# Query and key projections in two waves with held-back FFN steps between them, a second LayerNorm moved behind the next projections, and Sqrt on ScalarE in place of a Newton square root on VectorE

## The chip, the cores and the metric

One Trainium2 chip, all 8 cores, one launch. Each core computes one element of the batch (4096 rows of 1024 channels) and reads all weights itself; the cores don't talk to each other. The metric is the device time in microseconds (us) of the slowest core.

## What is computed

One transformer layer of the post-LayerNorm kind: linear attention (16 heads of 64, chunks of 128 rows, a running state S and z), residual and LayerNorm, then a mixture of 8 experts (each a 1024x1024 matrix, softmax gate, best two kept), residual and LayerNorm.

```python
q = phi(x @ Wq.T + bq); k = phi(x @ Wk.T + bk); v = x @ Wv.T + bv      # phi = elu + 1
for each chunk of 128 rows, per head:
    scores = tril(q k^T)
    out    = (scores v + q S) / sum(q * (cumsum(k) + z))
    S += k^T v;  z += sum(k)
x = layernorm(x + out @ Wo.T + bo)
gates = softmax(x @ gate_w.T + gate_b); top 2 of 8
x = layernorm(x + sum over the top 2 of gate_e * (x @ expert_w[e].T + expert_b[e]))
```

layernorm subtracts the mean and divides by sqrt(variance + 1e-5), with no learned scale.

## The kernel before

**Superchunks.** The 4096 rows of a core are worked through in 8 superchunks of 512 rows, numbered s = 0 to 7, each with four chunks of 128 rows, c = 0 to 3. All instructions are written out by hand, in one order per engine; `B.wait` and `B.waits` put semaphore waits into an engine's queue, and an engine runs its queue strictly in order. So the order in which the Python code calls `B.op` is the order in which each engine works.

**One superchunk** is four stages:

1. `proj_core` (lines 366 to 472). `proj_qk` computes Q, then K, transposed: for each of 8 slices k of the contraction, 8 matmuls (f = 0 to 7) of 512 columns, so that 64 matmuls (L377) fill all eight halves of the four PSUM tiles `quad` 0 to 3 (q0 to q3 in the rows). Only when the last slice is done does the evacuation begin: per f, ScalarE computes Exp (L393) and Relu (L398) of the half into `etmp` and `etmp2`, of which there are two each, and VectorE combines them (L404) into `qt_bf` or `kt_bf`. K needs the same eight halves, so its first matmul waits for Q's evacuation (line 375). Then K is transposed on TensorE (L426) and copied by VectorE (L435), and V is computed for four chunks (L449, bias L455) and evacuated by ScalarE (L465).
2. The scan over four chunks: `scores_part` (L554, masked by VectorE at L574), `sz_part` (state update, VectorE L626 to L644), `numden_div` (L670 and L675 on TensorE, L686 and L691 on VectorE), and, one chunk behind, `tail_chunk` (output projection L735, residual L755, first LayerNorm L761 to L770) and `tail_b` (transposes L787, their evacuation L795 on ScalarE, the gate: maximum L811, Exp L815, reciprocal L819, the bias term L859 and L871). `build_zmask` (ScalarE, L519) and `build_qz` (VectorE, L532) prepare masked copies of K and Q.
3. `x_stream(s + 1)`: the next superchunk's rows are loaded by POOL's queue and cast by VectorE (L361).
4. `ffn_drain`: 32 expert steps in the order expert 0 chunks 0 to 3, expert 1 chunks 0 to 3, and so on (e6,2 below is expert 6, chunk 2). A step is 16 matmuls of 512 columns (L886) into q0 or q1, alternately, and one VectorE instruction that multiplies by the gate and adds into `x1f` (L900). Then `ln2_out` (lines 929 to 956): for each of the four chunks, statistics (L937 to L943), inverse root (`rsqrt_dve`), normalisation (L947) and the output DMA from POOL's queue.

**The inverse root.** `rsqrt_dve` (lines 474 to 510) is 13 instructions on 128x1 tiles on VectorE: it adds epsilon (L482), guesses by integer arithmetic and makes two Newton steps (L485 to L506), and copies (L509). Both LayerNorms use it, 64 times in all.

**Weights.** There are 12 matrices of 2 MB in bf16 (0 Wq, 1 Wk, 2 Wv, 3 Wo, 4 to 11 the experts), and three buffers `wb` for them. `free_and_feed(mat)` frees a buffer when TensorE is done with a matrix and starts the next load into it, always three matrices ahead: the end of expert 5 starts the load of the next Wq, the end of expert 6 that of Wk, the end of expert 7 that of Wv. In superchunk 0 the matrices come as f32, in halves, through `wb2`, are cast by VectorE (L259) and ScalarE (L262) and stored to DRAM; from superchunk 1 on they are read back as bf16. Wq and Wk come in 8 pieces of 256 KB, one per slice k, even ones from SP's queue and odd ones from POOL's, and each queue waits until its last piece has landed before it issues the next:

```python
for k in range(KB):
    eng = "SP" if k % 2 == 0 else "POOL"
    cn = (f"dwl{slot}" if k % 2 == 0 else f"dwm{slot}")
    B.wait(eng, cn, B.val(cn))
    v = dma(eng, cn, wb[slot][:, k * 1024:(k + 1) * 1024],
            descr[m * 128:(m + 1) * 128,
                  k * 1024:(k + 1) * 1024])
    wpieces[m][k] = [(cn, v)]
```

Of the kernel before, what the change touches and what calls it, by code (L numbers as in the profile page):

```python
# [9 lines left out]
AF = mybir.ActivationFunctionType  # L10
# [11 lines left out]
KB = 8  # L22
# [66 lines left out]
def build():  # L89
# [276 lines left out]
    def proj_core(s):  # L366
        def proj_qk(mat, dstbf, donearr, bias_col):
            src = wb[wslot[mat]]
            vpe_f = [None] * KB
            for k in range(KB):  # L370
                B.waits("PE", wpieces[mat][k])
                B.wait("PE", "cdv", xt_cast[k])
                if k == 0:
                    for f in range(KB):
                        B.waits("PE", qwait(f // 2, (f % 2,)))
                for f in range(KB):
                    fn = lambda e, src=src, k=k, f=f: e.matmul(  # L377
                        quad[f // 2][:, (f % 2) * 512:(f % 2 + 1) * 512],
                        src[:, k * 1024 + f * 128: k * 1024 + (f + 1) * 128],
                        xt_bf[:, k * 512:(k + 1) * 512],  # L380
                        start=(k == 0), stop=(k == KB - 1))
                    if k == KB - 1:
                        vpe_f[f] = B.op("PE", fn, inc="cpe")
                    else:
                        B.op("PE", fn)
            for f in range(KB):
                qi, hh = f // 2, f % 2
# [3 lines left out]
                B.wait("ACT", "cpe", vpe_f[f])  # L391
# [18 lines left out]
            free_and_feed(mat)  # L410
# [299 lines left out]
    def tail_chunk(s, c, attn_evs):  # L710
# [57 lines left out]
        vrsq = rsqrt_dve(mnv[j][:, 1:2], rstd[j][:], rsq[j], [("cdv", vagg)])  # L768
        B.wait("DVE", "cdv", vrsq)
# [141 lines left out]
    ffn_qi = [0]  # L911

# [19 lines left out]
    def ln2_out(s):  # L932
        for c in range(CPS):
# [10 lines left out]
            vrsq2 = rsqrt_dve(mnv2[:, 1:2], rstd2[:], rsq[2], [("cdv", vagg)])  # L944
            B.wait("DVE", "cdv", vrsq2)
# [18 lines left out]
    fed_b2 = [False]  # L964
    for s in range(nsc if stage >= 1 else 0):
        proj_core(s)
        xtbf_free[0] = [("cpe", B.val("cpe"))]
# [36 lines left out]
        if stage >= 4:  # L1004
            ffn_drain(s)
# [4 lines left out]
        if stage >= 5:  # L1010
            ln2_out(s)
# [76 lines left out]
```

How the kernel before makes its waits and increments, by code:

```python
    def wait(self, eng, cname, val):  # L56
        if val is None or val <= 0:
            return
        w = self.waited[eng]
        if w.get(cname, 0) >= val:
            return
        w[cname] = val
        h = self.ctr[cname][0]
        self.streams[eng].append(lambda e, h=h, v=val: e.wait_ge(h, v))
# [14 lines left out]
        def run(e, fn=fn, h=h, k=k):  # L79
            fn(e).then_inc(h, k)
```

## Time and profile before

| what | value |
|---|---|
| median of 2 runs | 3003.82 us (2966.64 to 3041.0) |
| the profiled execution, whole | 2970.23 us |
| its span, first to last instruction, slowest core | 2968.7 us |
| spans of the other seven cores | 2951.6 to 2967.4 us |
| TensorE (PE) busy | 1916.2 us, 65% |
| VectorE (DVE) busy | 1106.4 us, 37% |
| ScalarE (ACT) busy | 405.4 us, 14% |
| DMA traffic | 304.01 MB, mean 102 GB/s |

The profile is of one execution, on core 5. All times in the rows are microseconds from the start of that core's span unless marked ns. PE is TensorE's matmuls, PEld its weight loads, DVE VectorE, ACT ScalarE, POOL and SP the two engines whose queues issue the DMAs. L377 is line 377 of the kernel. `out<-in` gives the tiles written and read, without buffer numbers. The bracket at the end of a timeline row is how long the engine stood idle before it, and which instruction ended that.

### The profile page before, as it was taken

The page shows a single profiled execution, that of the slowest core. Times are in us where ns is not written, and L with a number is a line of the kernel's source. Part 1 is how long each engine was busy: PE and PEld are TensorE (multiplying, and loading weights), DVE is VectorE, ACT ScalarE, POOL GpSimd, SP SyncE. Part 2 cuts the span into 40 slices and gives each one's busy share as a digit, 9 for nine tenths or more (in the row PEclk, how much of TensorE's full clock was granted, in tenths as well). Part 3 has the DMA queues.
Part 4 walks back from the last instruction along what each step waited for, and adds up shares of the span by engine and source line. Part 5 has one row for each costly group of instructions (what it writes and reads, how often), then busy time and mean ns, then how long its engine had stood idle before and what let it go on. Part 6 is the DMA issues. An engine that isn't in the chain of part 4 may idle for free.

```text
span 2968.7 us, 27823 instructions; the slowest of 8 cores (2951.6 to 2968.7 us)
## 1 busy us (share of the span) xinstructions
PE 1916.2 (65%) x10144; PEld 926.1 (31%) x10144; DVE 1106.4 (37%) x2224; ACT 405.4 (14%) x525; POOL 142.4 (5%) x265
## 2 busy tenths in 40 slices
PE   2355545565796549774696648964597646966495
PEld 0132222232342324332242323423243322423242
DVE  0233312433343433534334333434334333343434
ACT  1321110221003100131002200031001310022000
POOL 1000000100000000100000000000001000000000
PEclk8676777876897669886797768986698767977698
DMA  6630365410342113420243113420134202431031
GB/s 170 221 114 15 138 231 221 153 65 8 117 162 91 57 55 127 160 74 12 85 147 137 50 35 115 151 99 36 57 142 142 79 8 92 147 131 50 36 114 57
DMA packets 63356, 304.01 MB, mean 102 GB/s; under 512 B 8172, under 2 KB 8428, under 8 KB 43766
## 3 DMA queue, kind: packets, MB, share of 16 engines
q1 hardware_dynamic: 34326, 163.80, 16.6%
q0 software_dynamic: 28896, 138.43, 12.6%
q8 instruction: 83, 1.36, 0.2%
q14 instruction: 51, 0.42, 0.1%
HBM read 260.26 MB, written 41.94 MB: 102 GB/s over the span
## 4 chain that ended last, share of the span: by engine, by line
PE 52%; DVE 18%; DMA 10%; issue 10%; ACT 8%; DVEq 1%; POOL 0%; ACTq 0%; SPq 0%; POOLq 0%
PE q L886 27%; PE q L735 6%; DMA wb<-ewT 4%; PE q L449 4%; PE q L377 4%; DMA xtl<-xT 3%; PE q L741 2%; PE q L455 2%; ACT etmp L393 2%; PE q L554 2%; PE q L787 1%; ACT wb L262 1%; DVE x1f L755 1%; DVE x1f L871 1%; DVE S_f L626 1%
## 5 line engine op out<-in xcount | busy, mean ns | idle before, releaser
L886 PE MATMUL q<-wb,x1t_bf 128*128 128x512 bf16 x4096 | 927.4, 391 | 134.9 <-DVE x1f L900 63.6
L886 PEld LDWEIGHTS q<-wb,x1t_bf 128*128 128x128 bf16 x4096 | 408.6, 100 | 656.6 <-issue 201.6
L900 DVE SCALAR_TENSOR_TENSOR x1f<-q,w_all,x1f 128x1024 f32<-128x1024 f32 x256 | 328.2, 1283 | 546.5 <-PE q L886 546.5
L377 PE MATMUL q<-xt_bf,wb 128*128 128x512 bf16 x1024 | 245.4, 404 | 216.8 <-ACT etmp L398 165.0
L735 PE MATMUL q<-wb,attnTb 128*128 128x512 bf16 x512 | 172.9, 513 | 79.2 <-ACT attnTb L726 79.2
L377 PEld LDWEIGHTS q<-xt_bf,wb 128*128 128x128 bf16 x1024 | 103.9, 103 | 357.7 <-issue 253.3
L393 ACT ACTIVATE etmp<-q,bqc_s 128x512 f32<-128x512 f32 x64 | 45.2, 707 | 986.9 <-PE q L377 899.2
L554 PE MATMUL q<-qt_bf,ktz 128*128 128x128 bf16 x512 | 53.3, 287 | 173.3 <-DVE qtz L532 173.3
L196 POOL DMA_DIRECT2D wb<-escr x126 | 67.1, 533 | 1759.4 <-PE q L886 782.3
L755 DVE TENSOR_TENSOR x1f<-q,x0c 128x1024 f32<-128x1024 f32 x32 | 39.2, 1224 | 287.4 <-PE q L741 287.4
L574 DVE TENSOR_TENSOR msc_bf<-q,maskT_f 128x1024 bf16<-128x1024 f32 x64 | 75.4, 1220 | 186.6 <-PE q L554 186.6
L787 PE MATMUL q<-id_f,x1f 128*128 128x128 f32 x256 | 58.7, 406 | 128.1 <-DVE x1f L770 75.3
L449 PE MATMUL q<-wb,xt_bf 128*128 128x512 bf16 x512 | 119.9, 388 | 19.5 <-DVE ktm_bf L435 19.5
L735 PEld LDWEIGHTS q<-wb,attnTb 128*128 128x128 bf16 x512 | 61.7, 125 | 183.0 <-issue 163.4
L554 PEld LDWEIGHTS q<-qt_bf,ktz 128*128 128x128 bf16 x512 | 46.2, 132 | 181.6 <-issue 181.6
L259 DVE CAST wb<-wb 128x4096 bf16<-128x4096 f32 x12 | 27.5, 2293 | 197.5 <-DMA wb<-ewT 104.9
L404 DVE SCALAR_TENSOR_TENSOR kt_bf<-etmp 128x512 bf16<-128x512 f32 x64 | 44.3, 693 | 148.3 <-ACT etmp L398 148.3
L519 ACT ACTIVATE ktz<-kt_bf,pmask_s 128x1024 bf16<-128x1024 bf16 x64 | 70.0, 1140 | 203.1 <-PE q L554 196.9
L795 ACT ACTIVATE x1t_bf<-q 128x1024 bf16<-128x1024 f32 x32 | 32.6, 1019 | 449.1 <-PE q L787 449.1
L787 PEld LDWEIGHTS q<-id_f,x1f 128*128 128x128 f32 x256 | 49.9, 222 | 135.2 <-issue 135.2
L426 PE MATMUL q<-id_bf,kt_bf 128*128 128x128 bf16 x256 | 36.6, 295 | 67.1 <-DVE kt_bf L404 67.1
L449 PEld LDWEIGHTS q<-wb,xt_bf 128*128 128x128 bf16 x512 | 48.4, 99 | 95.5 <-issue 45.0
(85 smaller groups left out, 1590.7 us busy)
## 6 DMA issues: line engine op xcount, KB each, us to landing
wb<-escr SPq DMA_DIRECT2D x70, 1024.0 KB, 5.0
wb<-escr POOLq DMA_DIRECT2D x70, 1024.0 KB, 7.0
wb<-ewT SPq DMA_DIRECT2D x16, 2048.0 KB
escr<-wb SPq DMA_DIRECT2D x12, 2048.0 KB, 8.2
xtl<-xT POOLq DMA_DIRECT2D x64, 256.0 KB, 3.3
x0c<-x POOLq DMA_DIRECT2D x32, 512.0 KB, 5.0
out<-osb POOLq DMA_DIRECT2D x32, 512.0 KB, 2.9
wb<-escr SPq DMA_DIRECT2D x56, 256.0 KB, 3.3
```

The lines of the kernel that those rows point to most:

```text
L196: return B.op(eng, lambda e, o=out_ap, i=in_ap: e.dma_start(o, i), inc=cname, k=16)
L377: fn = lambda e, src=src, k=k, f=f: e.matmul(quad[f // 2][:, (f % 2) * 512:(f % 2 + 1) * 512], src[:, k * 1024 + f * 128: k * 1024 + (f + ...
L393: va = B.op("ACT", lambda e, qi=qi, hh=hh, et=et, bc=bc: e.activation(et[:], quad[qi][:, hh * 512:(hh + 1) * 512], AF.Exp, bias=bc), inc=" ...
L449: B.op("PE", lambda e, src=src, k=k, c=c, qi=qi, hh=hh: e.matmul(quad[qi][:, hh * 512:(hh + 1) * 512], xt_bf[:, k * 512 + c * 128: k * 512 ...
L519: vkz = B.op("ACT", lambda e, c=c, par=par, mcol=mcol: e.activation(ktz[:].rearrange("p (h w) -> p h w", w=128)[:, par::2, :], kt_bf[:].re ...
L554: fn = lambda e, h=h, f=f, c=c, qi=qi, hh=hh: e.matmul(quad[qi][:, hh * 128:(hh + 1) * 128], ktz[:, h * 128:(h + 1) * 128], qt_bf[:, f * 5 ...
L574: vm = B.op("DVE", lambda e, half=half, qi=qi: e.tensor_tensor(msc_bf[:, half * 1024:(half + 1) * 1024].rearrange("p (h w) -> p h w", w=12 ...
L735: B.op("PE", lambda e, src=src, k=k, hh=hh, j=j: e.matmul(quad[0][:, hh * 512:(hh + 1) * 512], attnT_bfp[j][:, k * 128:(k + 1) * 128], src ...
L755: vres = B.op("DVE", lambda e, j=j, c=c: e.tensor_tensor(x1f[:, c * 1024:(c + 1) * 1024], quad[0][:], x0c[j][:], ALU.add), inc="cdv")
L787: fn = lambda e, f=f, c=c: e.transpose(quad[0][:, f * 128:(f + 1) * 128], x1f[:, c * 1024 + f * 128: c * 1024 + (f + 1) * 128], id_f32[:])
L886: fn = lambda e, src=src, k=k, c=c, qi=qi, hh=hh: e.matmul(quad[qi][:, hh * 512:(hh + 1) * 512], x1t_bf[:, c * 1024 + k * 128: c * 1024 + ...
L900: e.scalar_tensor_tensor(x1f[:, c * 1024:(c + 1) * 1024], quad[qi][:], w_all[:, c * 8 + e_i: c * 8 + e_i + 1], x1f[:, c * 1024:(c + 1) * 1 ...
```

## The change

Three things are changed.

- **Two waves.** `proj_qk` now computes the eight output blocks in two waves of four, both in q2 and q3. After a wave its four blocks are evacuated (`emit_phi`, the old code), and `ffn_drain` emits up to two expert steps.
- **Held-back steps and the second LayerNorm.** At the end of a superchunk, except the last, six expert steps are left in the queue (e6,2, e6,3 and e7,0 to e7,3); they come out in the next superchunk's projections, two after each of the first three waves. `ln2_out` of superchunk s is then called after the whole of `proj_core(s + 1)`, ahead of its scan.
- **Sqrt.** In both LayerNorms `rsqrt_dve` gives way to a Sqrt with epsilon as bias on ScalarE and a reciprocal on VectorE, with a wait in each direction.

```diff
@@ -367,28 +367,37 @@
...
+            for wv in range(2):
+                fs = range(wv * 4, wv * 4 + 4)
+                for k in range(KB):
+                    B.waits("PE", wpieces[mat][k])
+                    B.wait("PE", "cdv", xt_cast[k])
+                    if k == 0:
+                        for f in fs:
+                            B.waits("PE", qwait(2 + (f % 4) // 2, ((f % 4) % 2,)))
+                    for f in fs:
+                        fn = lambda e, src=src, k=k, f=f: e.matmul(
+                            quad[2 + (f % 4) // 2][
+                                :, ((f % 4) % 2) * 512:((f % 4) % 2 + 1) * 512],
+                            src[:, k * 1024 + f * 128: k * 1024 + (f + 1) * 128],
+                            xt_bf[:, k * 512:(k + 1) * 512],
+                            start=(k == 0), stop=(k == KB - 1))
+                        if k == KB - 1:
+                            vpe_f[f] = B.op("PE", fn, inc="cpe")
+                        else:
+                            B.op("PE", fn)
+                for f in fs:
+                    emit_phi(mat, dstbf, donearr, bias_col, f, vpe_f[f])
+                ffn_drain(s_cur[0], limit=2)
+            free_and_feed(mat)
+
+        def emit_phi(mat, dstbf, donearr, bias_col, f, vpe):
+            if True:
+                qi, hh = 2 + (f % 4) // 2, (f % 4) % 2
...
@@ -765,8 +773,13 @@
...
-        vrsq = rsqrt_dve(mnv[j][:, 1:2], rstd[j][:], rsq[j], [("cdv", vagg)])
-        B.wait("DVE", "cdv", vrsq)
+        B.wait("ACT", "cdv", vagg)
+        vsq = B.op("ACT", lambda e, j=j: e.activation(
+            sdev[j][:], mnv[j][:, 1:2], AF.Sqrt, bias=eps_c[:, 0:1]), inc="cac")
+        B.wait("DVE", "cac", vsq)
+        vrs = B.op("DVE", lambda e, j=j: e.reciprocal(rstd[j][:], sdev[j][:]),
+                   inc="cdv")
+        B.wait("DVE", "cdv", vrs)
...
@@ -941,8 +955,13 @@
...
-            vrsq2 = rsqrt_dve(mnv2[:, 1:2], rstd2[:], rsq[2], [("cdv", vagg)])
-            B.wait("DVE", "cdv", vrsq2)
+            B.wait("ACT", "cdv", vagg)
+            vsq = B.op("ACT", lambda e: e.activation(
+                sdev2[:], mnv2[:, 1:2], AF.Sqrt, bias=eps_c[:, 0:1]), inc="cac")
+            B.wait("DVE", "cac", vsq)
+            vrs = B.op("DVE", lambda e: e.reciprocal(rstd2[:], sdev2[:]),
+                       inc="cdv")
+            B.wait("DVE", "cdv", vrs)
...
@@ -962,8 +981,14 @@
...
     for s in range(nsc if stage >= 1 else 0):
+        s_cur[0] = s
         proj_core(s)
+        if pend_ln2[0] is not None and stage >= 5:
+            ffn_drain(pend_ln2[0])
+            ln2_out(pend_ln2[0])
+            pend_ln2[0] = None
...
@@ -1002,13 +1027,18 @@
...
-            ffn_drain(s)
+            hold = 6 if s + 1 < nsc else 0
+            ffn_drain(s, limit=max(0, len(ffnq) - hold))
...
-            ln2_out(s)
+            if s + 1 < nsc:
+                pend_ln2[0] = s
+            else:
+                ffn_drain(s)
+                ln2_out(s)
```

The waves' matmuls are L379 in the changed kernel, the expert steps L899 with L913 on VectorE, the transposes of K L434, V L457 and L463, the new Sqrts L777 (first LayerNorm) and L959 (second), their reciprocals L780 and L962, the normalisation of the second L966, the mask L582, masked K copies L527, V's evacuation L473 and the cast of S L649.

TensorE around the projections of a superchunk from the second on, before: the 32 expert steps (512 matmuls), Q and K (128), the transposes, V's first chunk and its bias.

```order
L886 MATMUL q<-wb,x1t_bf 128x512 x512
L377 MATMUL q<-xt_bf,wb 128x512 x128
L426 MATMUL q<-id_bf,kt_bf 128x128 x32
L449 MATMUL q<-wb,xt_bf 128x512 x16
L455 MATMUL q<-bv_s,ones_r 128x512 x2
```

And now, at the same place:

```order
L899 MATMUL q<-wb,x1t_bf 128x512 x416
L379 MATMUL q<-xt_bf,wb 128x512 x32
L899 MATMUL q<-wb,x1t_bf 128x512 x32
L379 MATMUL q<-xt_bf,wb 128x512 x32
L899 MATMUL q<-wb,x1t_bf 128x512 x32
L379 MATMUL q<-xt_bf,wb 128x512 x32
L899 MATMUL q<-wb,x1t_bf 128x512 x32
L379 MATMUL q<-xt_bf,wb 128x512 x32
L434 MATMUL q<-id_bf,kt_bf 128x128 x32
```

26 expert steps stand before Q; the other six stand in pairs behind the first wave of Q, the second wave of Q and the first wave of K, and nothing stands between the second wave of K and the transposes.

VectorE from the masked copy of Q to the cast of the state in chunk 0 of such a superchunk, before (the second LayerNorm stood ahead of Q's L404, outside this piece):

```order
L532 TENSOR_SCALAR qtz<-qt_bf,pmask_s 128x8x128 x2
L435 COPY ktm_bf<-q 128x1024 x4
L574 TENSOR_TENSOR msc_bf<-q,maskT_f 128x1024 x2
L626 TENSOR_TENSOR S_f<-q,S_f 64x16x64
L631 TENSOR_TENSOR S_f<-q,S_f 64x16
L644 CAST Sbf<-S_f 64x1040
```

And now, from the last chunk of that LayerNorm to the same cast:

```order
L951 BN_STATS lnst<-x1f 128x6
L953 BN_STATS lnst<-x1f 128x6
L957 BN_AGGR mnv<-lnst 128x2
L962 RECIPROCAL rstd<-sdev 128x1
L966 TENSOR_SCALAR osb<-x1f,mnv,rstd 128x1024
L582 TENSOR_TENSOR msc_bf<-q,maskT_f 128x1024 x2
L634 TENSOR_TENSOR S_f<-q,S_f 64x16x64
L639 TENSOR_TENSOR S_f<-q,S_f 64x16
L652 CAST Sbf<-S_f 64x1040
```

All four chunks of the second LayerNorm (five instructions each) now stand between the copies of K and the first mask of the scan.

ScalarE at the same place, now, with the semaphores waited for (cpe counts TensorE, cdv VectorE):

```order
L527 ACTIVATE ktz<-kt_bf,pmask_s 128x8x128 [waits cdv]
L527 ACTIVATE ktz<-kt_bf,pmask_s 128x8x128
L473 ACTIVATE vext_bf<-q 128x16x64 [waits cpe] x4
L959 ACTIVATE sdev<-mnv,eps_c 128x1 [waits cdv] x4
L527 ACTIVATE ktz<-kt_bf,pmask_s 128x8x128 [waits cpe]
L527 ACTIVATE ktz<-kt_bf,pmask_s 128x8x128
L649 ACTIVATE Sbf<-S_f 64x1040 [waits cdv]
```

The four Sqrts are new; they stand behind the evacuation of all four chunks of V and ahead of the masked copy of K for chunk 1.

## Rows read from the trace of the kernel before

**Rows 1.** The page: span, and DMA issues (KB each, median us to landing).

```profile
span 2968.7 us, 27823 instructions; the slowest of 8 cores (2951.6 to 2968.7 us)
...
wb<-escr POOLq DMA_DIRECT2D x70, 1024.0 KB, 7.0
```

**Rows 2.** Windows, expert steps and scan: length, busy PE, PEld, DVE, ACT, POOL, PEclk, DMA.

```profile
760.00:885.00 125.00, 115.82 (x515) 51.16 (x514) 45.00 (x41) 0.00 (x0) 10.16 (x20) 0.95 0.38 130
...
968.00:1102.00 134.00, 64.77 (x509) 38.89 (x507) 58.53 (x147) 20.52 (x27) 4.52 (x9) 0.65 0.14 51
```

**Rows 3.** Timeline of TensorE, superchunk 2: start, duration, instructions, idle time before.

```profile
884.88 13.97 PE L377 MATMUL q<-xt_bf,wb 128*128 128x512 bf16 x64 [1.61 <-DVE x1f L900]
916.80 16.42 PE L377 MATMUL q<-xt_bf,wb 128*128 128x512 bf16 x64 [17.95 <-ACT etmp L398]
...
942.17 2.85 PE L426 MATMUL q<-id_bf,kt_bf 128*128 128x128 bf16 x25 [0.89 <-DVE kt_bf L404]
...
965.43 1.98 PE L455 MATMUL q<-bv_s,ones_r 1*128 1x512 f32 x4
...
970.84 0.19 PE L670 MATMUL q<-vext_bf,msc_bf 128*128 128x65 bf16 x1 [1.01 <-ACT ktz L519]
```

**Rows 4.** Timeline of VectorE, the same stretch.

```profile
883.45 1.28 DVE L900 SCALAR_TENSOR_TENSOR x1f<-q,w_all,x1f 128x1024 f32<-128x1024 f32 x1 [2.17 <-PE q L886]
884.65 0.68 DVE L937 BATCH_NORM_STATS2 lnst<-x1f 128x6 f32<-128x512 f32 x1
...
908.70 1.29 DVE L404 SCALAR_TENSOR_TENSOR qt_bf<-etmp 128x512 bf16<-128x512 f32 x2
...
941.33 0.69 DVE L404 SCALAR_TENSOR_TENSOR kt_bf<-etmp 128x512 bf16<-128x512 f32 x1 [0.47 <-ACT etmp L398]
...
968.07 2.36 DVE L574 TENSOR_TENSOR msc_bf<-q,maskT_f 128x1024 bf16<-128x1024 f32 x2 [22.26 <-PE q L554]
...
972.47 0.21 DVE L686 RECIPROCAL rden<-q 128x8 f32<-128x8 f32 x1
```

**Rows 5.** Timeline of ScalarE, the same stretch.

```profile
909.48 0.69 ACT L393 ACTIVATE etmp<-q,bqc_s 128x512 f32<-128x512 f32 x1 [9.62 <-DVE qt_bf L404]
...
931.87 0.69 ACT L393 ACTIVATE etmp<-q,bkc_s 128x512 f32<-128x512 f32 x1 [15.21 <-PE q L377]
...
967.51 1.03 ACT L465 ACTIVATE vext_bf<-q 128x1024 bf16<-128x1024 f32 x1 [4.44 <-PE q L455]
```

**Rows 6.** Timeline of POOL's queue: first and fourth of its pieces of Wq.

```profile
856.24 0.54 POOL L196 DMA_DIRECT2D wb<-escr  x1 [13.35 <-PE q L886]
...
868.46 0.54 POOL L196 DMA_DIRECT2D wb<-escr  x1 [3.29 <-DMA wb<-escr]
```

**Rows 7.** Timelines of VectorE and ScalarE in the tail of chunk 0, superchunk 2.

```profile
993.21 0.21 DVE L766 BATCH_NORM_AGGREGATE mnv<-lnst 128x2 f32<-128x12 f32 x1
...
997.00 0.81 DVE L770 TENSOR_SCALAR x1f<-x1f,mnv,rstd 128x1024 f32<-128x1024 f32 x1
...
1006.53 0.17 DVE L811 TENSOR_REDUCE negm<-q 128x1 f32<-128x8 f32 x1 [2.49 <-PE q L807]
...
1006.85 0.27 ACT L815 ACTIVATE eg<-q,negm 128x8 f32<-128x8 f32 x1 [1.22 <-DVE negm L811]
...
1007.31 0.16 DVE L819 RECIPROCAL rg<-sg 128x1 f32<-128x1 f32 x1 [0.61 <-ACT eg L815]
```

**Rows 8.** Timeline of ScalarE: the only table load of the program.

```profile
44.36 1.28 ACT L262 ACT_TABLE_LOAD   x1 [44.36 <-DMA wb<-wqT]
45.65 3.62 ACT L262 ACTIVATE wb<-wb 128x4096 bf16<-128x4096 f32 x1
```

**Rows 9.** Timelines of VectorE and TensorE where superchunk 1 begins.

```profile
505.44 2.29 DVE L259 CAST wb<-wb 128x4096 bf16<-128x4096 f32 x1 [26.08 <-DMA wb<-ewT]
...
574.35 15.29 PE L377 MATMUL q<-xt_bf,wb 128*128 128x512 bf16 x64 [27.29 <-ACT etmp L398]
```

**Rows 10.** Timeline of ScalarE in superchunk 0: the cast of Wo's first half.

```profile
126.12 3.62 ACT L262 ACTIVATE wb<-wb 128x4096 bf16<-128x4096 f32 x1 [4.46 <-DMA wb<-woT]
```

More of the change, by code:

```diff
@@ L369, in proj_qk @@
             vpe_f = [None] * KB
[L370 to L387, printed above, removed]
+            for wv in range(2):
[24 more added lines that the diff above has]
+                qi, hh = 2 + (f % 4) // 2, (f % 4) % 2
                 et = e_tmp[f % 2]
@@ L390, in proj_qk @@
                 bc = bias_col[:, f:f + 1]
-                B.wait("ACT", "cpe", vpe_f[f])
+                B.wait("ACT", "cpe", vpe)
                 B.waits("ACT", etmp_free[f % 2])
@@ L409, in proj_qk @@
                 etmp2_free[f % 2] = [("cdv", vd)]
-            free_and_feed(mat)
         proj_qk(0, qt_bf, qt_done, bqc_s)
@@ L911, in build @@
     ffn_qi = [0]
+    s_cur = [0]
     def ffn_drain(s, limit=None):
@@ L964, in build @@
     fed_b2 = [False]
+    pend_ln2 = [None]
     for s in range(nsc if stage >= 1 else 0):
+        s_cur[0] = s
         proj_core(s)
+        if pend_ln2[0] is not None and stage >= 5:
+            ffn_drain(pend_ln2[0])
+            ln2_out(pend_ln2[0])
+            pend_ln2[0] = None
         xtbf_free[0] = [("cpe", B.val("cpe"))]
```

## The prediction

> **What bounds the kernel now.** I read four views in this order: the windows by stage, the timeline of TensorE for one whole superchunk, those of VectorE and ScalarE under it, and POOL's queue. The windows show two kinds of stage [rows 2]. In the expert steps TensorE is busy for 115.82 of 125 us at a granted clock of 0.95, nearly all of it at 2.4 GHz; a step costs 1.28 + 2.17 = 3.45 us [rows 4], and nothing but TensorE matters. In the scan it is busy for 64.77 of 134 us at 0.65, a mixture of 1.2 and 2.4 GHz: there one chain runs through TensorE, VectorE and ScalarE in turn, and every microsecond on it counts.
>
> Between them stand the projections. Q takes 13.97 us, then TensorE waits 17.95 us for the evacuation, and K takes 16.42 us instead of 13.97, since its first matmuls run at the lower clock after the wait [rows 3]. ScalarE's own work for Q would take some 10 us; it stood still for 9.62 us, because both temporaries were full and VectorE had not begun to combine them [rows 5]. VectorE was in the second LayerNorm of the superchunk before, from 884.65 to 908.70, 24.05 us or 6.01 per chunk, and only then came to L404 [rows 4]. So the wait belongs to two things, the LayerNorm ahead in VectorE's queue and the eight blocks that are freed only at the end.
>
> **Part 1, waves and held-back steps, superchunks 2 to 7.** Before: six steps earlier than the end of the experts, the step e6,1 is done at 883.45 - 0.16 - 6 x 3.45 = 862.6 (0.16 us is about the hop from TensorE to VectorE). From there to the end of K at 916.80 + 16.42 = 933.2 are 70.6 us. After: four waves of 13.97 / 2 = 6.98 and six steps of 3.45, 48.6 us. A wave's evacuation is covered: eight K blocks take from 931.87 to 941.33 + 0.69, 10.15 us [rows 4, 5], 1.16 for each block after the first, so four take about 5.5 us, under 6.9 us of expert steps that write q0 and q1. The VectorE parts of those steps queue behind the evacuation, but the next use of q0 and q1 is a wave away.
>
> The cover has one hole. Wq is loaded when expert 5 is done. Its pieces go one by one in each queue: POOL's first is issued at 856.24, its fourth at 868.46 [rows 6], 4.07 us apart, so the last pair lands at 872.5. Before, Q began 12 us later and saw none of it. Now its first wave begins at 862.6 and wants slices 6 and 7 at 862.6 + 6 x 0.87 = 867.8: a stall of 4.7 us. Wk is loaded from the end of e6,3 and wanted 19 us later (a wave, two steps, six slices), against four pieces of 4.07 = 16.3 us: hidden. Gain: 70.6 - 48.6 - 4.7 = 17.3 us.
>
> Behind the second wave of K only four blocks are left instead of eight, 4 x 1.16 = 4.6 us less, minus 0.9 because the evacuation of a shorter wave begins nearer to its end: 3.8 us gained before the last transposes [rows 3].
>
> **Part 2, the second LayerNorm moved.** VectorE is nearly idle during V (22.26 us before the mask [rows 4]), which looks like free room. But ScalarE's order puts the four Sqrts behind V's last evacuation, which ends at 967.51 + 1.03 = 968.5 [rows 5]. VectorE can do the statistics of chunk 0 and then waits under the whole of V; all else comes after, and ahead of the first mask, which started at 968.07. What that costs needs the length of a round trip. From VectorE to ScalarE the hop is 1006.85 - 1006.70 = 0.15; a small ScalarE instruction 0.27; the way back is not seen alone (the row behind Exp has another small read between), so 0.1; reciprocal 0.16; 0.1 more: 0.78 us in place of 997.00 - 993.42 = 3.58 [rows 7]. So a chunk takes 6.01 - 2.80 = 3.2 us. The first also pays a table load, 1.28 us with the next instruction 0.01 us behind it [rows 8]: 1.28, then 0.63 for Sqrt, way back and reciprocal, and 0.71 for the normalisation: 2.6 us. LayerNorm ends at 968.5 + 2.6 + 3 x 3.2 = 980.7, the mask starts 12.8 us late. VectorE's next recip, 972.47, was its own queue's time and not TensorE's (970.84) [rows 3, 4], so all 12.8 us are on the chain. Bounds: 0 if the Sqrts ran under V, which the queue's order forbids; 24 at the old 6.01 per chunk. I take 12.8. The output DMAs and the x0c loads behind them on POOL's queue come later too, but x0c is wanted some 20 us after that.
>
> **Part 3, Sqrt in the tails.** Gain 2.80 us per chunk on the chain. Cost: Exp (gate, and phi) is loaded; Sqrt needs a load, and the next Exp another. The load of rows 8 waited for its data like the instruction behind it, so I place both on the chain, 1.28 each. In chunk 0 of superchunks 1 to 7 the Sqrt finds its table loaded: 2.80 - 1.28 = 1.52; in the other chunks 2.80 - 2.56 = 0.24. Sum 2.2 us a superchunk, 1.0 in superchunk 0. Bounds per load: 0 (hidden ahead of a wait) and 2.3 (the load, and a pipe that must first empty for as long as the longest neighbour, 1.03 [rows 5]); 1.28 is the row itself. There are 65 new loads: 8 a superchunk and one at the end.
>
> A rule speaks against this part. The trace shows 1.28 us and then the next instruction at once [rows 8]. The Trainium skill (ScalarE: Activation LUTs, What ACT_TABLE_LOAD costs) gives the same 1.28 for the load but adds a drain of 1.38 us to every switch of set. By that rule my sum would be 65 x 1.38 = 90 us longer; the one load seen here fell on an idle engine, and no row shows a switch between two sets.
>
> **Sum.** Superchunks 2 to 7: 17.3 + 3.8 - 12.8 + 2.2 = 10.5 each, 63. Superchunk 1: the last cast of expert 7 ends at 507.7, then Wq's pieces, 4 x 4.07 + 0.5, one slice, three waves and six steps: 507.7 + 16.8 + 0.9 + 20.9 + 20.7 = 567.0 against 574.35 + 15.29 = 589.6 [rows 9]; 22.6 + 3.8 - 12.8 + 2.2 = 15.8. Superchunk 0 has no steps to fill with: its K ends about 8 us later, Wo's cast on ScalarE had 4.46 us of room [rows 10], so 3 us lost, 1 won in the tails. The last LayerNorm, at the open end: 4 x 2.80 - 1.28 = 9.9. Together 63 + 15.8 - 2 + 9.9 = 86.7 us. The profiled execution took 2970.2 us (span 2968.7 [rows 1]): 2970.2 - 86.7 = 2883.5, say 2884. The median of the runs shown, 3003.82, lies 34 us above it and is the middle of two runs 74 us apart; the forecast is for an execution like the profiled one.
>
> **Rivals.** A measurement of this kernel tells about 2% from no change, which is 60 us.
>
> (A) The switches cost more: ScalarE must empty before a load. For: loads now fall between copies of 1.03 us. Against: rows 8, and ScalarE mostly waits when a Sqrt comes. 65 x 1.03 = 67 us: 2951. By the rule of the Trainium skill named above it would be 2974.
>
> (B) The LayerNorm is not shortened by Sqrt: if a round trip with its waits costs what the 13 instructions did, the four chunks take 24 us, a mask 25 us late instead of 12.8, 7 x 12.5 = 87: 2971, no change. For: two engines and three waits per chunk. Against: the hop of 0.15 us.
>
> (C) Slower: the serial pieces of Wq and Wk. Let L be the time of one piece. Wq stalls its wave by 4L - 11.6, Wk by 4L - 19.1, together 8L - 30.7 once L is over 4.8. The gain is gone at a stall of 4.7 + 86.7 / 7 = 17.1, L = 6.0. At L = 7.0, the median of the larger loads [rows 1], the stall is 25.3, 20.6 more, 144 us, and with waits that long the lower clock returns in both first waves, 2.45 each [rows 3], 34 us: 3062. For: TensorE no longer leaves slack, and all cores load at once. Against: these are the same bytes at the same point after expert 5, and were 4.07 apart there.
>
> (D) The change doesn't do what it says: excluded by the order, where the steps stand in pairs between the waves.
>
> **How the numbers follow.** Forecast 2884 with a chance of 0.66, its own range 2850 to 2920 (hop and stall terms of 2 us per superchunk either way, and half the loads hidden); A 0.14; B 0.07; C 0.08; better than 2850, with loads hidden ahead of their waits (65 x 1.28 = 83 us: 2801), 0.05. The range 2845 to 2975 leaves out C and most of the last. The bound of 2% is 2911: faster 0.69 (most of the first, and the last), slower, over 3030, 0.1 (C, and 0.02 for A or B turning out worse than priced), same the rest, 0.21.
>
> **What would show it.** Right: TensorE without a wait for L407 between the waves; a first wave of Q of about 11.7 us and the other three of 7; the mask of chunk 0 about 12 us behind V's last evacuation; 65 more table loads of 1.28 us with a Sqrt or Exp directly behind; a superchunk of some 331 us instead of 342. Wrong: gaps of over 1 us beside the loads (A), a LayerNorm chunk of over 5 us in front of the mask (B), waits for weights in K's first wave (C).

## The result, and the profile after

| | before | after |
|---|---|---|
| median of all runs | 2969.91 us (10 runs) | 2902.95 us (11 runs) |
| the profiled execution, whole | 2970.23 us | 2906.11 us |
| its span, slowest core | 2968.7 us | 2904.6 us |
| VectorE busy | 1106.4 us | 980.3 us |
| ScalarE busy | 405.4 us | 507.6 us |

The ratio is 0.9767, 95% interval 0.9756 to 0.9779: 2.3% faster, some 69 us. The forecast was 2884 us with a range of 2845 to 2975. In some executions of any of these kernels the cores of one die, four of the eight, show a lower granted clock and the time is some per cent longer; the medians of the table hold them, and the ratios and the times told for the experiments leave them out.

The slowest core of the profiled execution is now core 1, and the rows below are of that core unless another is named. I read the same views in the same order. First the groups that answer to the projections, by line (busy us, mean ns; then idle time before them and what ended it). Before:

```profile
L377 PE MATMUL q<-xt_bf,wb 128*128 128x512 bf16 x1024 | 245.4, 404 | 216.8 <-ACT etmp L398 165.0 <-DVE wb L259 34.1 <-DVE x1f L900 11.2
...
L670 PE MATMUL q<-vext_bf,msc_bf 128*128 128x65 bf16 x512 | 36.5, 195 | 20.8 <-ACT ktz L519 20.8
```

And now:

```profile
L379 PE MATMUL q<-xt_bf,wb 128*128 128x512 bf16 x1024 | 243.4, 395 | 137.2 <-DMA wb<-escr 49.5 <-ACT etmp L407 41.2 <-DVE wb L259 37.8
...
L678 PE MATMUL q<-vext_bf,msc_bf 128*128 128x65 bf16 x512 | 42.5, 206 | 110.6 <-DVE msc_bf L582 97.4 <-ACT ktz L527 13.2
...
L828 ACT ACT_TABLE_LOAD x32 | 41.1, 1283 | 44.9 <-DVE negm L824 44.9
...
L777 ACT ACT_TABLE_LOAD x25 | 32.1, 1283 | 277.5 <-DVE mnv L774 277.5
...
L959 ACT ACT_TABLE_LOAD x8 | 10.3, 1283 | 119.7 <-DVE mnv L957 119.6
```

TensorE's wait for the evacuations shrank from 165 us to 41.2 us, all of it in superchunk 0, where no held-back steps stand between the waves. Two new waits took its place: 49.5 us for the weights' pieces, 29.0 of it ahead of superchunk 1, and 97.4 us for the mask in front of L678. There are 65 new table loads, 32 + 25 + 8, as counted.

TensorE in superchunk 2, which answers to [rows 3]. Before, the first matmuls of V and the scores of chunks 0 and 1 stood here:

```profile
945.32 3.78 PE L449 MATMUL q<-wb,xt_bf 128*128 128x512 bf16 x16 [0.30 <-DVE ktm_bf L435]
...
967.35 1.07 PE L554 MATMUL q<-qt_bf,ktz 128*128 128x128 bf16 x16
...
975.33 1.87 PE L554 MATMUL q<-qt_bf,ktz 128*128 128x128 bf16 x16 [3.35 <-DVE qtz L532]
```

Now:

```profile
858.89 5.34 PE L379 MATMUL q<-xt_bf,wb 128*128 128x512 bf16 x24
864.40 1.02 PE L379 MATMUL q<-xt_bf,wb 128*128 128x512 bf16 x4 [0.17 <-DMA wb<-escr]
866.58 1.02 PE L379 MATMUL q<-xt_bf,wb 128*128 128x512 bf16 x4 [1.16 <-DMA wb<-escr]
867.44 7.07 PE L899 MATMUL q<-wb,x1t_bf 128*128 128x512 bf16 x32
...
902.36 7.07 PE L379 MATMUL q<-xt_bf,wb 128*128 128x512 bf16 x32
...
917.73 3.76 PE L457 MATMUL q<-wb,xt_bf 128*128 128x512 bf16 x16 [0.30 <-DVE ktm_bf L443]
...
939.74 1.07 PE L562 MATMUL q<-qt_bf,ktz 128*128 128x128 bf16 x16
...
962.27 1.86 PE L562 MATMUL q<-qt_bf,ktz 128*128 128x128 bf16 x16 [3.71 <-DVE qtz L540]
```

From 858.89 to the end of K at 909.43 are 50.5 us for four waves and six steps; nothing waits for an evacuation, and the last two pieces of Wq cost 1.3 us here (3.3 us in the median of superchunks 2 to 7). V starts 8.3 us behind K's end, 12.1 before. But from the scores of chunk 0 (939.74) to those of chunk 1 are 22.5 us, 7.98 before. What fills them stands in ScalarE's and VectorE's timelines, first ScalarE's:

```profile
939.90 1.03 ACT L473 ACTIVATE vext_bf<-q 128x1024 bf16<-128x1024 f32 x1 [4.44 <-PE q L463]
940.95 1.28 ACT L959 ACT_TABLE_LOAD   x1
942.24 0.29 ACT L959 ACTIVATE sdev<-mnv,eps_c 128x1 f32<-128x1 f32 x1
945.39 0.29 ACT L959 ACTIVATE sdev<-mnv,eps_c 128x1 f32<-128x1 f32 x1 [2.86 <-DVE mnv L957]
```

and VectorE's:

```profile
942.64 0.16 DVE L962 RECIPROCAL rstd<-sdev 128x1 f32<-128x1 f32 x1 [22.55 <-ACT sdev L959]
...
945.79 0.17 DVE L962 RECIPROCAL rstd<-sdev 128x1 f32<-128x1 f32 x1 [0.49 <-ACT sdev L959]
...
951.15 0.81 DVE L966 TENSOR_SCALAR osb<-x1f,mnv,rstd 128x1024 f32<-128x1024 f32 x1 [2.04 <-DMA out<-osb]
...
955.03 2.35 DVE L582 TENSOR_TENSOR msc_bf<-q,maskT_f 128x1024 bf16<-128x1024 f32 x2
```

VectorE stood for 22.55 us under the whole of V with the statistics of chunk 0 ready, because the Sqrt was queued behind V's last evacuation. After that a chunk takes 3.15 us. In front of chunk 2 a 2.04 us wait for an output buffer comes on top, to which the first experiment returns. It differs from core to core: from the scores of chunk 0 to those of chunk 1 the median is 22.5 us on this core and 20.7 to 21.8 on the other seven.

### The profile page after: what moved, and what is told of

It is laid out like the page before. It is cut to its first block, busy times and chain, and to the rows that moved or that the text cites. A ratio compares the mean times of both kernels' runs of the same rounds, so it can differ in the third digit from the quotient of the medians.

```text
span 2904.6 us, 26453 instructions; the slowest of 8 cores (2878.5 to 2904.6 us)
## 1 busy us (share of the span) xinstructions
PE 1931.4 (66%) x10144; PEld 934.9 (32%) x10144; DVE 980.3 (34%) x1456; ACT 507.6 (17%) x654; POOL 142.7 (5%) x265
## 4 chain that ended last, share of the span: by engine, by line
PE 54%; DMA 15%; DVE 13%; ACT 9%; issue 8%; DVEq 1%; POOL 0%; ACTq 0%; SPq 0%; POOLq 0%
PE q L899 26%; PE q L743 6%; PE q L379 5%; DMA wb<-ewT 4%; DMA wb<-escr 4%; PE q L457 4%; DMA xtl<-xT 3%; PE q L749 2%; PE q L463 2%; PE q L800 2%; PE q L562 2%; ACT L828 1%; DVE x1f L763 1%; DMA out<-osb 1%; DVE x1f L884 1%
## 5 line engine op out<-in xcount | busy, mean ns | idle before, releaser
L899 PE MATMUL q<-wb,x1t_bf 128*128 128x512 bf16 x4096 | 936.6, 392 | 106.7 <-DVE x1f L884 58.1
L899 PEld LDWEIGHTS q<-wb,x1t_bf 128*128 128x128 bf16 x4096 | 410.1, 101 | 632.9 <-issue 181.1
L913 DVE SCALAR_TENSOR_TENSOR x1f<-q,w_all,x1f 128x1024 f32<-128x1024 f32 x256 | 328.1, 1283 | 477.2 <-PE q L899 477.2
L379 PE MATMUL q<-xt_bf,wb 128*128 128x512 bf16 x1024 | 243.4, 395 | 137.2 <-DMA wb<-escr 49.5
L743 PE MATMUL q<-wb,attnTb 128*128 128x512 bf16 x512 | 181.3, 532 | 79.8 <-ACT attnTb L734 79.8
L379 PEld LDWEIGHTS q<-xt_bf,wb 128*128 128x128 bf16 x1024 | 101.6, 101 | 273.7 <-issue 166.3
L457 PE MATMUL q<-wb,xt_bf 128*128 128x512 bf16 x512 | 124.3, 399 | 14.8 <-DVE ktm_bf L443 14.8
L800 PE MATMUL q<-id_f,x1f 128*128 128x128 f32 x256 | 60.5, 416 | 103.2 <-DVE x1f L783 62.8
L743 PEld LDWEIGHTS q<-wb,attnTb 128*128 128x128 bf16 x512 | 63.6, 129 | 190.1 <-issue 175.1
L678 PE MATMUL q<-vext_bf,msc_bf 128*128 128x65 bf16 x512 | 42.5, 206 | 110.6 <-DVE msc_bf L582 97.4
L413 DVE SCALAR_TENSOR_TENSOR qt_bf<-etmp 128x512 bf16<-128x512 f32 x64 | 44.2, 692 | 153.4 <-ACT etmp L407 153.4
L854 PE MATMUL q<-id_bf,w_bfs 128*8 128x128 bf16 x32 | 8.5, 264 | 122.5 <-DVE w_bfs L847 122.5
L527 ACT ACTIVATE ktz<-kt_bf,pmask_s 128x1024 bf16<-128x1024 bf16 x64 | 69.9, 1140 | 89.9 <-PE q L562 83.7
L582 DVE TENSOR_TENSOR msc_bf<-q,maskT_f 128x1024 bf16<-128x1024 f32 x64 | 75.3, 1218 | 30.4 <-PE q L562 30.4
```

The source lines that it names most:

```text
L379: fn = lambda e, src=src, k=k, f=f: e.matmul(quad[2 + (f % 4) // 2][:, ((f % 4) % 2) * 512:((f % 4) % 2 + 1) * 512], src[:, k * 1024 + f * ...
L413: e.scalar_tensor_tensor(d[:, f * 512:(f + 1) * 512], et[:], 1.0, et2[:], ALU.min, ALU.add), inc="cdv")
L457: B.op("PE", lambda e, src=src, k=k, c=c, qi=qi, hh=hh: e.matmul(quad[qi][:, hh * 512:(hh + 1) * 512], xt_bf[:, k * 512 + c * 128: k * 512 ...
L527: vkz = B.op("ACT", lambda e, c=c, par=par, mcol=mcol: e.activation(ktz[:].rearrange("p (h w) -> p h w", w=128)[:, par::2, :], kt_bf[:].re ...
L582: vm = B.op("DVE", lambda e, half=half, qi=qi: e.tensor_tensor(msc_bf[:, half * 1024:(half + 1) * 1024].rearrange("p (h w) -> p h w", w=12 ...
L743: B.op("PE", lambda e, src=src, k=k, hh=hh, j=j: e.matmul(quad[0][:, hh * 512:(hh + 1) * 512], attnT_bfp[j][:, k * 128:(k + 1) * 128], src ...
```

## The experiments

Every experiment ran on all 8 cores. "us" is the span of the profiled execution or, where said so, the whole time of a run. A stage named "scores 0 to scores 1" runs from the first score matmul of chunk 0 to that of chunk 1; the medians of stages are over superchunks 2 to 7 on the slowest core. The kernel before was run again beside each of three groups of experiments and took 2965 to 2972 us in the median, so spans of different groups compare to within some 7 us.

**Newton back, the rest as changed.** In both LayerNorms:

```diff
-            B.wait("ACT", "cdv", vagg)
-            vsq = B.op("ACT", lambda e: e.activation(
-                sdev2[:], mnv2[:, 1:2], AF.Sqrt, bias=eps_c[:, 0:1]), inc="cac")
...
+            vrsq2 = rsqrt_dve(mnv2[:, 1:2], rstd2[:], rsq[2], [("cdv", vagg)])
+            B.wait("DVE", "cdv", vrsq2)
```

> The changed kernel with the Newton square root back in both LayerNorms; waves, held-back steps and the moved LayerNorm stay. Theory (the exposed part of the second LayerNorm comes from the place of the four Sqrts in ScalarE's queue, behind V's last evacuation): without them VectorE works through chunks 0 and 1 under V, until chunk 2 needs an output buffer whose DMA stands on POOL's queue behind the weight load that waits for the end of V. From the scores of chunk 0 to those of chunk 1 I expect about 18.5 us where the changed kernel has 20.7 to 22.5; the tails lose about 1.3 us a superchunk and the last LayerNorm 9 us at the end: 2900 us, within 10 of the changed kernel. Rival (the LayerNorm's own length counts, whatever the queue): 24 us of it stand in front of the mask, 32 us from scores to scores, 7 x 10 us and the 18 of the tails and the end more: 2990 us.

Measured: ratio 0.9866 (0.9797 to 0.9936), span 2933.7 us, 29 us slower than the changed kernel where I expected no more than 10. The theory and the rival both missed: scores 0 to scores 1 is 26.7 us (24.7 to 25.2 on the other seven cores), between 18.5 and 32. The reason is in VectorE's timeline of that kernel (core 3; L956 is its normalisation):

```profile
928.01 0.81 DVE L956 TENSOR_SCALAR osb<-x1f,mnv,rstd 128x1024 f32<-128x1024 f32 x1 [0.18 <-DVE rstd L517]
...
951.08 0.81 DVE L956 TENSOR_SCALAR osb<-x1f,mnv,rstd 128x1024 f32<-128x1024 f32 x1 [17.29 <-DMA out<-osb]
```

and POOL's queue beside it:

```profile
938.88 0.53 POOL L196 DMA_DIRECT2D wb<-escr  x1 [29.71 <-PE q L463]
939.41 1.06 POOL L196 DMA_DIRECT2D out<-osb  x2
```

Chunks 0 and 1 were indeed done under V, and chunk 2 then waited 17.29 us for its output buffer: the mechanism was the one named, the size was not. The DMA that frees that buffer could not be issued before the weight load of 1 MB in front of it on the queue, which waits for the end of V. Then it took 11 us beside that load and the output DMA of chunk 1, which was issued with it; the median of such a DMA in this kernel is 3.0 us. So a queue that is shared with weight loads cost twice, once by its order and once by the longer transfer; how much of the 11 us each neighbour carries was not separated. The same thing in small is the 2.04 us of the changed kernel. Beside the 4.2 us a superchunk that this makes against the changed kernel, the tails take 126.1 us against 124.6 and the open end is 9.8 us longer, as expected; 3.0 us a superchunk are given back between the last gate and the scores, and why was not separated.

**Sqrt alone, on the kernel before.** The two edits on Sqrt of the change, nothing else.

> The kernel before with only the Sqrt part of the change, in both LayerNorms. Theory: the second LayerNorm stands ahead of Q's evacuation on VectorE, 24 us before, about 14 now, so TensorE's wait between Q and K falls from 18 us to about 10, the floor set by ScalarE's eight blocks; 8 us in 7 superchunks, 1.3 in the tails of each and 9 at the end: some 74 us less than before, 2896 us, as much as the whole change. Rival (the gain of the change is that of the waves and the filling steps, and the table loads eat what Sqrt saves): the wait stays near 18 us, 2955 to 2970 us.

Measured: ratio 0.9769 (0.9682 to 0.9856), span 2904.2 us, as the whole change (2904.6), and the theory's number was 2896. Its runs took 2897, 2906 and 2923 us, so "as much" holds to about 1%. TensorE at K, which answers to the second of [rows 3]:

```profile
909.02 15.49 PE L377 MATMUL q<-xt_bf,wb 128*128 128x512 bf16 x63 [9.37 <-ACT etmp L398]
```

The wait is 9.37 us instead of 17.95. So half of the wait that the waves remove belonged to the LayerNorm's length. What the waves and the move add to Sqrt is then nothing that these runs can tell. From the last gate to V's start are 178.1 us here and 165.7 in the changed kernel, a gain of 12.4 a superchunk; V takes 22.8 and 22.6; and scores 0 to scores 1 takes 8.0 here and 22.5 there, so the moved LayerNorm gives 14.5 back. Superchunk 1 is 7 us shorter in the changed kernel, and superchunk 0 and the open end together are 4 us longer.

**LayerNorm under V.** On the changed kernel; `ln2_out` behind `proj_core` goes.

```diff
         for c in range(CPS):
+            if pend_ln2[0] is not None:
+                ln2_out(pend_ln2[0], (c,))
             qi = c % 2
             B.waits("PE", qwait(qi))
             B.waits("PE", wready[2])
...
-    def ln2_out(s):
-        for c in range(CPS):
+    def ln2_out(s, chunks=range(CPS)):
+        for c in chunks:
```

> The changed kernel with chunk c of the second LayerNorm emitted ahead of chunk c of V, on all engines, instead of behind the whole of V. Theory (the LayerNorm is exposed only because of where its Sqrts stand, and V has room for it): from the scores of chunk 0 to those of chunk 1 takes 8 us again as before the change, 12.7 to 14.5 us less, in 7 superchunks, 89 to 100 us: 2810 us. Rival (ScalarE and VectorE are delayed by each other during V, and V's evacuations then hold up TensorE, which uses two tiles in turn): V grows by 3 us per chunk and the gain is 0 to 3 us a superchunk: 2880 to 2903 us.

Measured: ratio 0.9433 (0.9343 to 0.9523), span 2804.8 us; the theory's number was 2810. Scores 0 to scores 1 is 7.98 us again in superchunks 1 to 6 and 8.07 in the last, as before the change, and V takes 22.6 us as in the changed kernel. ScalarE (core 4; L475 is V's evacuation, L961 Sqrt):

```profile
911.75 1.03 ACT L475 ACTIVATE vext_bf<-q 128x1024 bf16<-128x1024 f32 x1 [2.15 <-PE q L465]
912.67 0.28 ACT L961 ACTIVATE sdev<-mnv,eps_c 128x1 f32<-128x1 f32 x1
917.22 1.03 ACT L475 ACTIVATE vext_bf<-q 128x1024 bf16<-128x1024 f32 x1 [4.26 <-PE q L465]
```

The Sqrts stand in the gaps between V's evacuations. This is 100 us for moving one call, more than the whole change gained, and it shows that the 12.8 us of the sum were a matter of queue place.

**Free pieces.** On the changed kernel, one semaphore for each of the eight pieces of Wq and Wk.

```diff
-                    cn = (f"dwl{slot}" if k % 2 == 0 else f"dwm{slot}")
+                    cn = f"dp{k}"
                     B.wait(eng, cn, B.val(cn))
```

> The changed kernel with one semaphore for each of the eight pieces of Wq and Wk, so that no piece waits for the one before it on its queue. Theory (the wait of Q's first wave for its weights comes from that chain): the first wave of Q falls from 8.6 to 12 us to 7 us, and Q of superchunk 1 starts some 8 us earlier: 20 to 30 us less, 2878 us. Rival (the bandwidth sets when the last piece lands, and the pieces only crowd each other): less than 5 us, 2900 us.

Measured: ratio 0.9676 (0.9609 to 0.9743), span 2877.9 us against an expected 2878. Waves and steps take 48.51 us in the median, where the changed kernel has 51.83 and the prediction's sum without a stall 48.6. All four waves of superchunk 2 read like this one (core 3), without a wait:

```profile
854.98 7.07 PE L380 MATMUL q<-xt_bf,wb 128*128 128x512 bf16 x32
```

**Both together.**

> Both changes together that helped alone: the second LayerNorm's chunks ahead of V's chunks, and a semaphore for each piece of Wq and Wk. Theory (the two costs lie in different places and add up): Q's and K's waves with their six steps take 48.5 us as with the free pieces alone, the scores of chunk 1 follow those of chunk 0 after 8 us as with the LayerNorm under V alone: 2806 less 22 us, 2784 us. Rival (one hides part of the other): not below 2795 us.

Measured: ratio 0.9390 (0.9367 to 0.9413), runs of 2781 to 2790 us against an expected 2784: they add up. From the scores of chunk 0 to those of chunk 1 are 7.98 us, and waves and steps take 48.51.

**One wave in superchunk 0.** The same, and:

```diff
-            for wv in range(2):
-                fs = range(wv * 4, wv * 4 + 4)
+            nw = 1 if s_cur[0] == 0 else 2
+            per = KB // nw
+            pl = lambda f: f if nw == 1 else 4 + f % 4
+            for wv in range(nw):
+                fs = range(wv * per, wv * per + per)
```

> The same, with superchunk 0, which has no held-back steps, back in the form with one wave of eight blocks. Theory (the first scores of superchunk 0 came at 172.3 us instead of 166.7 because its waves have nothing between them): 3 to 6 us less than with two waves there, 2780 us. Rival (superchunk 0 is bound by the f32 weights all the same, and the difference is that of two cores and runs): no difference, within 2 us.

Measured: ratio 0.9360 (0.9343 to 0.9376), runs of 2772 to 2779 us. About 9 us less by the ratios, whose intervals overlap, and 7 by the medians of the runs; 3 to 6 were expected. The first scores come at 162.9 us instead of 168.9, and the waits for weights in the rest of superchunk 0 and at the start of superchunk 1 differ too; which of these carries the rest I did not separate.

**Newton, with the LayerNorm under V and free pieces.**

> The kernel with LayerNorm under V and free pieces, with the Newton square root back in both LayerNorms. Theory (where the LayerNorm stands right, Sqrt is worth only its place at the open end and a little elsewhere, since in the tails seven or eight table loads of 1.28 us take what it saves): 9 us at the end, 1.6 us a superchunk in the tails, about 2.5 us a superchunk because four Newton chunks take 24 us against 22 us of V: some 37 us slower, 2820 us. Rival (Sqrt is the larger part of the gain, as the kernel with Sqrt alone suggested with its 2904 us): 60 to 80 us slower, 2850 to 2865 us.

Measured: ratio 0.9479 (0.9458 to 0.9500), runs of 2805 to 2814 us, 26 us slower than its twin with Sqrt, the kernel of "Both together" (0.9390), where 37 were expected and the rival said 60 to 80. The stages of the two spans, 2812.5 and 2788.7 us, say where: 9.8 us behind the last gate, at the open end; 7.1 us in superchunks 2 to 7 together, of which 0.7 us a superchunk, in the median, in front of chunk 1's scores; 8.9 us in superchunk 0, where the first scores come at 175.4 us instead of 168.9; and 1.9 us given back in superchunk 1. In the tails there is next to nothing: from chunk 1's scores to chunk 3's gate transpose are 125.6 us with Newton and 125.4 with Sqrt in the median, 126.1 and 125.4 in the mean.

**No held-back steps.** The twin with Sqrt, and:

```diff
-            hold = 6 if s + 1 < nsc else 0
+            hold = 0
```

> The kernel with LayerNorm under V and free pieces, with no expert steps held back: two waves, nothing between them. Theory (the six steps cover four evacuations of four blocks): three waits of about 4.1 us in each of 7 superchunks, 86 us slower, 2870 us. Rival (two waves alone shorten the wait enough, since the first blocks are free before the last is needed): under 30 us slower, 2810 us.

Measured: runs of 2901.5 us (the profiled one, span 2899.9) and 2921.7, too few for an interval. The span is 111 us above the twin's, where the theory said 86 and the rival under 30. A wave in it (core 7), and the window of that wave:

```profile
884.75 8.75 PE L380 MATMUL q<-xt_bf,wb 128*128 128x512 bf16 x32 [4.33 <-ACT etmp L408]
```

```profile
884.70:893.50 8.80, 8.75 (x32) 3.50 (x32) 0.69 (x1) 0.50 (x1) 0.00 (x0) 0.81 0.00 0
```

The wait is near the expected 4.1 us, but the wave behind it takes 8.75 us instead of 7.07 at a granted clock of 0.81, so after the wait TensorE worked in part at 1.2 GHz. There are 21 such waits of 4.33 or 4.38 us in superchunks 1 to 7, and 3 x (4.38 + 1.7) is 18.2 us a superchunk; from the last gate to V's start the two kernels differ by 18.7. V and the tails are each 0.8 us shorter here, which leaves 17 us in each of superchunks 2 to 7; superchunks 0 and 1 together lose 9 us, and the open end gains 1: together the 111. So a held-back step pays twice here, by the wait and by the clock.

**Tables loaded early.** On the kernel with one wave in superchunk 0, in `tail_chunk` and `tail_b`:

```diff
             sdev[j][:], mnv[j][:, 1:2], AF.Sqrt, bias=eps_c[:, 0:1]), inc="cac")
+        B.op("ACT", lambda e: e.activation(
+            pre_s[:], eps_c[:], AF.Exp, bias=eps_c[:, 0:1]), inc="cac")
...
             accum_out=sg[j][:]), inc="cac")
+        if c < CPS - 1:
+            B.op("ACT", lambda e: e.activation(
+                pre_s[:], eps_c[:], AF.Sqrt, bias=eps_c[:, 0:1]), inc="cac")
```

> The kernel with LayerNorm under V, free pieces and one wave in superchunk 0, with two 128x1 activations more per tail, whose results nobody reads: an Exp right behind the Sqrt, and a Sqrt right behind the gate's Exp (not in chunk 3). Theory (each table load stands on the tail's chain because it is issued only when its own instruction is, and costs 1.28 us there; ScalarE stands idle for several us before it): seven loads a superchunk leave the chain, 9.0 us, in seven superchunks, and a few in superchunk 0, which the f32 weights bound: 60 to 68 us less than 2775, 2710 us. Rival (the added activations delay ScalarE's next instruction by 1.6 us each and give it back, or the loads are not on the chain): 2765 us or more.

Measured: ratio 0.9113 (0.9098 to 0.9127), runs of 2702 to 2707 us against an expected 2710. ScalarE around the gate of chunk 0, superchunk 2 (core 1; L838 is the gate's Exp, L842 the added Sqrt, L657 the next work):

```profile
936.55 0.27 ACT L838 ACTIVATE eg<-q,negm 128x8 f32<-128x8 f32 x1 [1.22 <-DVE negm L834]
...
936.92 1.28 ACT L842 ACT_TABLE_LOAD   x1
938.22 0.29 ACT L842 ACTIVATE pre_s<-eps_c 128x1 f32<-128x1 f32 x1
945.22 1.07 ACT L657 ACTIVATE Sbf<-S_f 64x1040 bf16<-64x1040 f32 x1 [6.70 <-DVE S_f L647]
```

The gate's Exp starts at once when its input is there, the load falls into the time behind it, and ScalarE still waits 6.70 us for its next work. The tails take 115.9 us instead of 125.3, which is 9.4 us a superchunk where the theory had 9.0.

**Only the Exp loaded early.**

> The same with only the Exp behind the Sqrt. Theory: four loads a superchunk leave the chain, 5.1 us, 36 to 40 us less than 2775 in all, 2737 us. Rival (as above): 2765 us or more.

Measured: ratio 0.9209 (0.9193 to 0.9226), runs of 2731 to 2734 us against an expected 2737. The tails take 119.8 us. Both numbers were counted load by load at 1.28 us and came out to within 8 us: the loads of the tails were on the chain.

## Why the prediction was right, point by point

The direction and the size were right: 86.7 us were forecast for the profiled execution, 64.1 came (2968.7 - 2904.6), and the median lies 19 us above the forecast, inside the likeliest case's own range, 2850 to 2920. A quarter of the forecast gain is missing all the same, and part of it is hidden by a term that came out better than forecast. By its steps:

| term, us per superchunk 2 to 7 | forecast | measured (medians) |
|---|---|---|
| waves and steps, less the Wq stall | +17.3 | +19.0 |
| fewer blocks before V | +3.8 | +3.8 |
| V's first matmuls | 0 | -0.6 |
| LayerNorm in front of the mask | -12.8 | -14.5 |
| Sqrt in the tails | +2.2 | +0.3 |
| sum of these | +10.5 | +8.0 |
| superchunks 2 to 7 together | +63 | +51.4 |
| superchunk 1, once | +15.8 | +10.4 |
| superchunk 0, once | -2 | -6.1 |
| the last tails and LayerNorm | +9.9 | +8.4 |
| all | +86.7 | +64.1 |

The lower rows are differences of the two spans (core 5 before, core 1 after); six times the medians' sum falls 3 us short of the 51.4. The sum also has a credit that it did not earn by itself: it gives the waves all of the 17.95 us between Q and K, and Sqrt, with the LayerNorm where it was, would have removed half of them. That Sqrt alone could be worth as much as the three parts together the prediction does not see.

**The wait between Q and K** came out as said: from superchunk 1 on no evacuation is waited for between the waves. That half of it belonged to the LayerNorm's length is shown by Sqrt alone (9.37 us left).

**The Wq hole** was there, in the place and by the cause named, and smaller than 4.7 us: the pieces came 3.56 us apart in the superchunk read above instead of 4.07. Its whole size is what free pieces gave, 3.3 us in the median. Wk had a stall of 0.22 us in superchunk 2, so "hidden" was just about true. At a piece time of 3.56 us rival C, which needed 6.0, is out; in the worst of the six superchunks waves and steps took 55.7 us, a stall of 7.2 where C needed 17.1 to undo the gain.

**The LayerNorm in front of the mask** was 12.7 us on core 5 (20.67 - 7.98), where the forecast says 12.8 (its own 980.7 less 968.07 is 12.6), and 14.5 on core 1, the slowest, where the output buffer was late. The sum had the output DMAs come later at no cost; that step was short by 1.7 us, and the experiment with Newton shows how far it can fail. Rival B is out: a chunk takes 3.15 us against 3.2 forecast.

**The tails** are the term that was mis-sized. In chunk 1 of superchunk 2 the path through ScalarE is exact; ScalarE's rows, then VectorE's:

```profile
1013.57 1.28 ACT L777 ACT_TABLE_LOAD   x1 [10.91 <-DVE mnv L774]
1014.87 0.29 ACT L777 ACTIVATE sdev<-mnv,eps_c 128x1 f32<-128x1 f32 x1
```

```profile
1013.28 0.21 DVE L774 BATCH_NORM_AGGREGATE mnv<-lnst 128x2 f32<-128x12 f32 x1
1015.26 0.16 DVE L780 RECIPROCAL rstd<-sdev 128x1 f32<-128x1 f32 x1 [1.77 <-ACT sdev L777]
1015.53 0.81 DVE L783 TENSOR_SCALAR x1f<-x1f,mnv,rstd 128x1024 f32<-128x1024 f32 x1
```

1015.53 - 1013.49 = 2.04 us, forecast 0.78 + 1.28 = 2.06. The sum held TensorE's own time in the tails fixed, and it was not. The windows of chunks 1 and 2 in the tails, before and after (columns as in [rows 2]); the kernel before first:

```profile
1000.60:1035.00 34.40, 16.21 (x129) 10.08 (x130) 14.96 (x37) 5.43 (x7) 0.53 (x1) 0.65 0.05 16
1035.00:1066.40 31.40, 16.32 (x130) 10.06 (x131) 12.69 (x32) 3.36 (x5) 0.00 (x0) 0.66 0.00 1
```

then the changed one:

```profile
984.20:1019.50 35.30, 17.03 (x130) 10.44 (x131) 13.03 (x25) 8.29 (x10) 0.53 (x1) 0.60 0.05 16
1019.50:1050.90 31.40, 16.64 (x129) 10.23 (x129) 10.72 (x20) 6.22 (x8) 0.00 (x0) 0.61 0.00 1
```

The granted clock fell from 0.65 and 0.66 to 0.60 and 0.61, and the same matmuls are busy for 0.8 and 0.3 us longer. The output projection in all, L743, is busy for 181.3 us where L735 was for 172.9. From the scores of chunk 1 to the last gate TensorE is busy for 62.6 us in the median, 60.7 before: these 1.9 us are as much as the term is short by. Why the clock was lower stays open. The idle time of 1.28 us that each load adds on TensorE is an obvious candidate, but loading both tables early, which takes it away, left the busy time at 62.8 us (63.3 in that kernel's twin) and the output projection at 181.6, so it can explain a small part at most. Nor did it fall everywhere: between the scores of chunks 2 and 3 it is 0.60 in two of the six superchunks and 0.65 in four, 0.65 in all before; from the scores of chunk 3 to the last gate it is 0.60 in five and 0.58 in one, where it was 0.63 in four and 0.58 in two. That the loads cost the chain is shown, since loading both tables early won 9.4 us a superchunk.

**Table loads** cost 1.28 us each and nothing more. The load of the rows above at 940.95 begins 0.02 us after a copy of 1.03 us ends, and the Sqrt 0.01 us behind the load. The load at 1013.57, on an engine that had been idle, has its Sqrt 0.02 us behind it. So rival A is out. The drain of 1.38 us that the Trainium skill (ScalarE: Activation LUTs, What ACT_TABLE_LOAD costs) adds to a switch is not seen here, neither behind a busy engine nor an idle one; by that rule the sum would have been 90 us longer, an estimate from the page's figure.

**Superchunk 0** lost 6.1 us where the sum had 2, nearly all of it before the first scores (166.7 us before, 172.3 after). Its K ended not 8 but 22 us later, at 126.9 us instead of 104.7, with three waits for evacuations, of 26.8, 4.4 and 10.0 us, where one of 30.1 stood. V started only 4.8 us later, at 147.6 instead of 142.7, because both kernels wait in front of it. The experiment with one wave there won 7 to 9. **Superchunk 1** lost against the sum at its start: TensorE ended the first wave at 534.4, where I had 525.4. Of these 9 us 5.4 are the time by which superchunk 0 ran late (the last cast ended at 513.1 instead of 507.7), and the rest comes with the first piece of Wq, which took 8.7 us beside the store of the last expert, where the sum had 4.07.

## What to carry to other kernels

Before work is moved to another place in one engine's program, look at where it lands in the queues of all engines it touches: the same LayerNorm cost 13 to 14.5 us a superchunk behind V's last evacuation on ScalarE and nothing between the evacuations, and its output DMA cost up to 17 us behind a weight load. When table loads stand on a serial chain, issue the load early with an instruction that does nothing else; here seven small activations a superchunk, 56 in all, took the ratio from 0.936 to 0.911, some 70 us. And when several edits come together, try each alone: Sqrt by itself was worth the whole change, and the other two edits cancelled each other, until the LayerNorm stood in the right place: then they were worth 99 us over Sqrt alone (2904.2 to 2804.8).

## What the runs showed that I had not expected

An idle time of 4.33 us on TensorE was enough to bring the next 32 matmuls from 7.07 to 8.75 us. With steps between the waves and free pieces the projections of superchunks 2 to 7 ran at a granted clock of 1.00 on all eight cores; in the changed kernel, where the first wave still waits for pieces, core 1 had 1.00 in four of these six and 0.94 and 0.97 in the others. A 512 KB output DMA issued right behind a 1 MB weight load, together with a second one, took 11 us where the median was 3.0. And Sqrt on ScalarE with one or two table loads costs about as much in the tails as 13 dependent VectorE instructions of 0.16 us: in the three pairs of kernels that differ in this alone, 125.4 us against 125.6, 124.6 against 126.1 and 125.6 against 124.9. Only with the loads taken off the chain does it win.
